# The out-projection in halves of sixteen bits, and the cuts of weights and rows shared out anew among three engines

## The reference

```python
x = x + attention(layernorm(x), ctx, ctx, Wq, Wk, Wv, Wfc, bfc)   # 32 heads of 16, 8 groups of keys; "@ Wfc.T + bfc" is the out-projection
x = x + ffn(layernorm(x), gate_weight, gate_w, up_w, down_w, sh_gate_w, sh_up_w, sh_down_w)

def ffn(h):                                   # h: 2048 rows of 512
    scores = softmax(h @ gate_weight.T)       # 8 experts in 4 groups, the best 2 groups, in them the best 2 experts
    wmat = weights of the two chosen experts, 0 for the others
    routed = sum over e of wmat[:, e] * ((silu(h @ gate_w[e].T) * (h @ up_w[e].T)) @ down_w[e].T)      # width 352
    shared = (silu(h @ sh_gate_w.T) * (h @ sh_up_w.T)) @ sh_down_w.T                                    # width 704
    return routed + shared
```

## Time and profile before

| | us |
|---|---|
| device time, median of 3 runs | 774.12 (771.83 to 774.58) |
| profiled execution, its own time | 773.04 |
| span of its instructions | 771.3 |
| TensorE busy in the span | 748.0 (97%) |
| VectorE | 567.5 (74%) |
| ScalarE | 424.4 (55%) |
| GpSimd | 267.4 (35%) |

### The profile page before, as it was taken

How to read it: one execution, slowest core, us unless ns; L and a number is a source line. 1 busy time by engine, 2 the same in 40 slices (tenths; PEclk the granted TensorE clock), 3 DMA queues, 4 the chain that set the end, 5 groups by cost and what they waited for, 6 DMA issues and landing times.

```text
span 771.3 us, 15970 instructions
## 1 busy us (share of the span) xinstructions
PE 748.0 (97%) x5151; PEld 404.5 (52%) x5152; DVE 567.5 (74%) x1194; ACT 424.4 (55%) x860; POOL 267.4 (35%) x222
## 2 busy tenths in 40 slices
PE   6998999999999999999999999999999999999997
PEld 4553533444444335666655656555555555555554
DVE  5777779999999977887689886555555555446767
ACT  3666568988888875776624543343434343323231
POOL 3263007999995303657000101111111111016331
PEclk9999989999999999999999999999999999999999
DMA  9898846575655799996678556777777779549995
GB/s 331 336 406 252 252 158 202 170 208 170 181 178 158 248 356 331 367 381 224 192 203 243 138 134 160 178 180 177 180 177 177 180 180 216 128 110 280 306 259 164
DMA packets 161336, 171.04 MB, mean 222 GB/s; under 512 B 103616, under 2 KB 117440, under 8 KB 160768
## 3 DMA queue, kind: packets, MB, share of 16 engines
q1 hardware_dynamic: 149724, 128.36, 57.0%
q0 software_dynamic: 10960, 40.90, 17.1%
...
## 4 chain that ended last, share of the span: by engine, by line
PE 77%; DVE 13%; DMA 5%; issue 2%; ACT 2%; SPq 1%; ACTq 0%; DVEq 0%
PE psum L1500 31%; PE psum L1512 17%; DVE sb_rows L1732 6%; PE psum L1430 5%; PE psum L1349 5%; PE psum L1239 4%; PE psum L1335 4%; PE psum L1263 3%; DMA sb_weights<-in_wdn 2%; PE psum L1215 2%; DMA sb_weights<-in_x 1%; PE psum L1366 1%; PE psum L1448 1%; PE psum L1220 1%; DMA x_dram<-sb_rows 1%
## 5 line engine op out<-in xcount | busy, mean ns | idle before, releaser
L1500 PE MATMUL psum<-sb_weights,sb_rows 128*128 (+1 forms) x1608 | 250.8, 313 | 0.0
L1500 PEld LDWEIGHTS psum<-sb_weights,sb_rows 128*128 128x128 f16 x1608 | 157.3, 98 | 91.1 <-DMA sb_rows<-xnT_dram 0.3
L1732 DVE TENSOR_REDUCE sb_rows<-psum 128x4 f32<-128x1024 f32 x128 | 149.9, 1215 | 5.4 <-PE psum L1263 5.4
L1054 ACT ACTIVATE sb_weights<-psum 128x512 f32<-128x512 f32 x256 | 139.2, 595 | 23.5 <-PE psum L1335 20.5
L1512 PE MATMUL psum<-sb_weights,sb_hT 128*128 (+1 forms) x630 | 147.2, 379 | 0.0
...
L1512 PEld LDWEIGHTS psum<-sb_weights,sb_hT 128*128 128x128 f16 x630 | 61.6, 98 | 64.8
L1128 ACT ACTIVATE psum<-psum 128x352 f32<-128x352 f32 x71 | 31.8, 448 | 114.4 <-DVE psum L1986 104.0
L1335 PE MATMUL psum<-sb_weights 50*128 50x512 f16 x256 | 87.0, 390 | 2.3 <-ACT sb_weights L1054 1.4
L1349 PE MATMUL psum<-sb_weights 128*32 128x256 f32 x1024 | 83.1, 397 | 0.3
L1263 PE MATMUL psum<-sb_weights 48*128 48x256 f16 x512 | 71.8, 275 | 0.7 <-DVE sb_rows L1732 0.7
L1986 DVE SCALAR_TENSOR_TENSOR psum<-psum,sb_inv_now,sb_h 128x352 f32<-128x352 f32 x39 | 23.1, 593 | 49.0 <-issue 40.1
...
...
## 6 DMA issues: line engine op xcount, KB each, us to landing
...
slot_y<-sb_rows SPq DMA_DIRECT2D x39, 256.0 KB, 2.3
...
x_dram<-sb_rows SPq DMA_DIRECT2D x24, 256.0 KB, 4.2
q_parts<-sb_weights SPq DMA_DIRECT2D x16, 256.0 KB, 4.0
sb_rows<-in_x POOLq DMA_DIRECT2D x16, 256.0 KB, 5.4
```

The source lines that it names most:

```text
L1054: nc.scalar.activation(probs[G % 2][:, kt, pair * 512:(pair + 1) * 512], bank[4 + f % 2], ACT.Exp, scale=exp_by[n]).then_inc(exp_done, 1)
L1500: mm = nc.tensor.matmul(bank[GU_BANKS[par][which]][:, 0:F], x_T[:, xp * D + k * P:xp * D + (k + 1) * P], gu(wp, k, which), start=(k == 0 a ...
L1732: nc.vector.tensor_reduce(to[:, :, j // UB, :, j % UB, qt], psum[:, banks[qt] * 512:(banks[qt] + 2) * 512] .rearrange("p (a h k) -> p a h ...
```

## The change

1. **The out-projection in float16.** Wfc (4 tiles of 128x512) is loaded early; its scale comes from a sum of squares that GpSimd makes in the projections' time (8 products and sums of 128x512 and smaller), ScalarE squares the values (`v_square`) for a scale of attention's rows; `cut_fc` (GpSimd, attention) cuts Wfc in 4 x 3 instructions. `ot_evac` writes the high part with the scale, VectorE makes the low part (`out_low`, one instruction of 128x512 for a tile), and TensorE does 12 float16 products for a tile: eight with the high part, then, behind a wait for `out_low`, four with the low part. The residual sum becomes one instruction with a factor.
2. **Held experts.** Four instead of five: GpSimd cuts 12 halves in attention instead of 10. The remaining eight halves all go to VectorE (`second_part` in the tiles 2, 4, 5, 7, 8, 10, 11 and 13). SyncE loads them.
3. **Normed rows.** `cut_rows` goes from VectorE to GpSimd, which also issues the store of the rows; the shared down matrices are cut by GpSimd around the tiles 12 and 14.
4. **Shared down scales by squares.** The last two `dn_abs_max` go; GpSimd sums the squares of the two matrices instead (`shared_sum`, 10 instructions each) between its bias sums, and VectorE takes the result in `shared_tops`.
5. **The seam.** The first two `ot_transpose` are issued two steps earlier, the last `normalise` stands inside the first `residual_norm`, bias sums go in pairs of tiles, the ring has one turn of five buffers and three more, and the register loads come before attention.

The diff, cut to what matters (places in SBUF, the ring's order, the squares of Wfc and `load_scales` are left out):

```diff
-HELD = 5
+HELD = 4
 CUTS_P2 = CUTS - 2 * HELD
+HELD_TILES = (2, 4, 5, 7, 8, 10, 11, 13)
+SHARED_TILES = (12, 14)
...
+                    if (n, l) == (2, 0):
+                        sp.dma_start(wfc_words, wfcT.rearrange("p k n -> p (k n)")).then_inc(fc_ld, 16)
...
+                if u == 12:
+                    sp.wait_ge(fc_cut, CUT_SEEN + FC_STEPS * KD)
+                    for c in range(SH):
+                        load_shared_down(c)
+                for i in {12: (0, 1), 13: (2, 3, 4)}.get(u, ()):
...
+            bias_order = list(range(1, TILES // 2)) + [0]
+            squares, SUM_STEPS, SUMS_SEEN = units[:, 0:DN_W], 10, SQUARE_SEEN + 2 * KD + 7
+            def shared_sum(c):
+                raw, done = dn_raw((NE + c) % 3), SUMS_SEEN + SUM_STEPS * c
+                nc.gpsimd.tensor_tensor(squares, raw, raw, ALU.mult).then_inc(fc_square, 1)
+                n, done = DN_W // 2, done + 1
+                pool.wait_ge(fc_square, done)
+                while n > NF:
+                    nc.gpsimd.tensor_tensor(squares[:, 0:n], squares[:, 0:n], squares[:, n:2 * n], ALU.add).then_inc(fc_square, 1)
+                    n, done = n // 2, done + 1
+                    pool.wait_ge(fc_square, done)
+                nc.gpsimd.tensor_tensor(dn_sums[:, c, :], squares[:, 0:NF], squares[:, NF:2 * NF],
+                                        ALU.add).then_inc(fc_square, 1)
+                pool.wait_ge(fc_square, done + 1)
...
-                if i >= 2:
-                    pool.wait_ge(xb_st[i % 2], i // 2 * 16)
-                nc.gpsimd.dma_start(xb_sb[i % 2], x_tiles[bias_order[i]]).then_inc(xb_ld[i % 2], 16)
+                if i > 0:
+                    pool.wait_ge(xb_st, i * 16)
...
+            def cut_fc(k):
+                scale = w_scale[:, FC_COL:FC_COL + 1].broadcast_to([P, D])
+                nc.gpsimd.tensor_tensor(wfc16[:, k, 0, :], wfc_raw[k], scale, ALU.mult).then_inc(fc_cut, 1)
+                pool.wait_ge(fc_cut, CUT_SEEN + FC_STEPS * k + 1)
+                nc.gpsimd.tensor_tensor(wfc_raw[k], wfc_raw[k], scale, ALU.mult).then_inc(fc_cut, 1)
+                pool.wait_ge(fc_cut, CUT_SEEN + FC_STEPS * k + 2)
+                nc.gpsimd.tensor_tensor(wfc16[:, k, 1, :], wfc_raw[k], wfc16[:, k, 0, :], ALU.subtract).then_inc(fc_cut, 1)
+            pool.wait_ge(w_fc, 32)
             load_x(0)
             for t in range(TILES):
+                if t < KD:
+                    cut_fc(t)
                 if t < CUTS_P2:
-                    pool.wait_ge(nm_done, t + 3)
+                    pool.wait_ge(nm_done, t * 5 // 6 + 3)
                     cut_weights(t)
-                if t + 1 < TILES:
-                    load_x(t + 1)
-                add_bias(t)
-            def dn_second(e, count, pieces):
+                if t in (TILES - 3, TILES - 1):
+                    c = (t - TILES + 3) // 2
+                    pool.wait_ge(sh_ld, 16 * SH)
+                    shared_sum(c)
+                if t == TILES - 1:
+                    nc.gpsimd.memset(units[:, 0:2 * FP], 0.0).then_inc(h_zero, 1)
+                if t % 2 == 0:
+                    add_bias(t // 2)
+                elif t + 1 < TILES:
+                    load_x(t // 2 + 1)
...
-            pool.wait_ge(attn_done, UNITS * UG)
-            pool.wait_ge(dn_max_done, NE + SH)
-            for h in range(3):
-                load_held(h)
-            for c in range(CUTS_P2, CUTS):
-                h = c - CUTS_P2
-                if h % 2 == 0:
-                    scale_weights(c)
-                    second_part(c)
-                else:
-                    pool.wait_ge(gu_cut_v, h // 2 + 1)
-                if h + 3 < 2 * HELD:
-                    load_held(h + 3)
-            for c in range(SH):
-                dn_second(NE + c, c + 1, [dn_raw((NE + c) % 3)])
...
+            def cut_rows(t):
+                s = t % 2
+                pool.wait_ge(lnt_evac, t + 1)
+                nc.gpsimd.tensor_tensor(ln16[s][:, D:2 * D], lnT[s], ln16[s][:, 0:D], ALU.subtract).then_inc(ln16_done, 1)
+                pool.wait_ge(ln16_done, t + 1)
+                nc.gpsimd.dma_start(xnT_dram[t], ln16[s]).then_inc(lnt_stored[s], 16)
+            for t in range(TILES):
+                cut_rows(t)
+                if t + 2 in SHARED_TILES:
+                    c = SHARED_TILES.index(t + 2)
+                    dn_scaled_part(NE + c, c + 1, dn_raw((NE + c) % 3))
+                if t + 1 in SHARED_TILES:
+                    c = SHARED_TILES.index(t + 1)
+                    dn_low(NE + c, c + 1, dn_raw((NE + c) % 3))
...
+            def v_square(n):
+                nc.scalar.activation(bank[5], bank[5], ACT.Square,
+                                     accum_out=half_max[:, 2 * V_COLS + n:2 * V_COLS + n + 1]).then_inc(v_free, 1)
...
-                nc.scalar.copy(oT[s], bank[s][:].rearrange("p (k t) -> p k t", k=KD)).then_inc(ota_evac, 1)
+                nc.scalar.activation(oT[s][:, 0], bank[s][:].rearrange("p (k t) -> p k t", k=KD), ACT.Copy,
+                                     scale=out_scale(t)).then_inc(ota_evac, 1)
...
+            ot_evac(1, 1)
             attn_out(UNITS * UG - 1)
             nc.scalar.activation(warm, ident[:, 0:TPB], ACT.Sqrt)
+            ot_evac(2, 0)
             for t in range(2):
-                ot_evac(t + 1, (t + 1) % 2)
...
-                if t - 2 < 2 * HELD:
-                    first_part(t - 2)
-                if t == 2:
+                if t in HELD_TILES:
+                    first_part(HELD_TILES.index(t))
...
-                    mm = nc.tensor.matmul(bank[2 + s][:], oT[s][:, k, :], wfc_sb[:, k, :],
-                                          start=(k == 0), stop=(k == KD - 1))
+                    for wp in range(2):
+                        nc.tensor.matmul(bank[2 + s][:], oT[s][:, 0, k, :], wfc16[:, k, wp, :],
+                                         start=(k == 0 and wp == 0), stop=False)
+                pe.wait_ge(ot_cut, t + (LOW_SEEN + 1))
+                for k in range(KD):
+                    mm = nc.tensor.matmul(bank[2 + s][:], oT[s][:, 1, k, :], wfc16[:, k, 0, :],
+                                          start=False, stop=(k == KD - 1))
...
+            out_project(0, 0)
+            pair_transpose(LAST - 1)
+            ot_transpose(2, 2, 0)
+            out_project(1, 1)
+            pe.wait_ge(dn_max_done, NE + 1)
...
+            def out_low(t):
+                dve.wait_ge(ota_evac, t + 1)
+                nc.vector.scalar_tensor_tensor(oT[t % 2][:, 1], bank[t % 2][:].rearrange("p (k t) -> p k t", k=KD), out_scale(t),
+                                               oT[t % 2][:, 0], ALU.mult, ALU.subtract).then_inc(ot_cut, 1)
+            def shared_tops():
+                dve.wait_ge(fc_square, SQUARE_SEEN + 2 * KD + 7 + 10 * SH)
+                link(nc.vector.tensor_reduce(dn_max[:, NE:NE + SH], dn_sums, AX.X, ALU.max))
+                nc.vector.tensor_scalar(dn_max[:, NE:NE + SH].bitcast(I32), dn_max[:, NE:NE + SH].bitcast(I32), 0.5, float(127 << 22),
+                                        ALU.mult, ALU.add).then_inc(dn_max_done, 1)
+            out_low(0)
+            shared_tops()
+            out_low(1)
+            dve.wait_ge(scale_done, 1)
+            link(nc.vector.tensor_scalar(fc_inv, w_inv[:, V_COLS:V_COLS + 2], w_inv[:, FC_COL:FC_COL + 1], X_SCALE * X_SCALE,
+                                         ALU.mult, ALU.mult))
...
-            dn_abs_max(2 * UG)
-            dn_abs_max(2 * UG + 1)
-            normalise(UNITS * UG - 2)
-            def cut_rows(t, s):
-                dve.wait_ge(lnt_evac, t + 1)
-                nc.vector.scalar_tensor_tensor(ln16[s][:, D:2 * D], bank[4 + s], X_SCALE, ln16[s][:, 0:D],
-                                               ALU.mult, ALU.subtract).then_inc(ln16_done, 1)
...
-                nc.vector.tensor_tensor(x2_sb[s], bank[2 + s][:], residual, ALU.add).then_inc(x2_done, 1)
+                nc.vector.scalar_tensor_tensor(x2_sb[s], bank[2 + s][:], fc_inv[:, t // EARLY:t // EARLY + 1], residual,
+                                               ALU.mult, ALU.add).then_inc(x2_done, 1)
                 dve.wait_ge(x2_done, t + 1)
                 link(nc.vector.bn_stats(stats[:, 0, :], x2_sb[s]))
                 link(nc.vector.bn_aggr(mv[:, s, :], stats[:, 0, :]))
                 nc.vector.tensor_scalar(var_e[:, 0:1], mv[:, s, 1:2], EPS, None, ALU.add).then_inc(var_done, 1)
-                if not (isinstance(t, int) and t < 2):
-                    cut_rows(t - 2, s)
+                if t == 0:
+                    normalise(UNITS * UG - 2)
+                elif t + 1 < TILES:
+                    out_low(t + 1)
...
-                residual_norm(t, t % 2, t // 2)
-                if t % 2 == 1 and t < 2 * HELD + 2:
-                    second_part(t - 2)
-            cut_rows(TILES - 2, 0)
+                if t > 2:
+                    residual_norm(t, t % 2, t // 2)
+                if t in HELD_TILES:
```

(1 more changed line is left out.)

308 lines of the change are left out of this document (171 added, 137 removed).

## The result

The changed kernel takes 788.27 us (median of 4 runs, 786.88 to 791.05) beside 772.98 for the kernel before: ratio 1.0207, 95% interval 1.0177 to 1.0238, slower by 15 to 16 us. The forecast was 778.0 in a range of 767 to 786. The sign of the likeliest case was right, its size (5.0) a third of what came, and the time lies outside the range. The profiled execution took 787.37, its span is 785.6, 14.3 more than before.

A forecast was written before the change was run, and what follows sets the result against it. TensorE was taken to bound the token stage, VectorE close behind; +6.7 (GpSimd wait) - 4.2 (token stage) + 1.0 (tail) - 0.5 (register loads) + 2.0 (clock) = +5.0 on 773.04, so 778.0, range 767 to 786.

The forecast's parts named there:

- the likeliest case: Whole kernel: the terms' sum, +5.0 on 773.04, so 778.0, own range 774.5 to 782; chance 0.45.
- TensorE in the token stage: Out-projection: twelve float16 products take 2.59 instead of 3.44 to 3.55, a tile needs 4.3, 0.9 less.
- VectorE from the fifth tile on: Token stage: VectorE late next, 3.64 a tile plus eight held cuts of 1.59; 71.0 against 75.3, -4.2.
- Rival C: Token stage: `cut_rows` on GpSimd holds up held cuts, each staying at 2.6; 8 x 1.0, 786; chance 0.15.
- A: Seam: GpSimd not last if sums give back 2.7, pairs 3.6, landings 3.1; end 285.9, time 767; chance 0.18.
- B: Seam: both landings at 3.8, GpSimd ends at 293.6, no clock loss; 774, same; chance 0.22.
- GpSimd through attention: Attention to seam: GpSimd's new work ends at 295.3, VectorE waits, x2 of tile 0 at 296.8 instead of 290.07, +6.7.
- The last landing: GpSimd ahead of the second `shared_sum`: last load's landing uncovered, 3.1 and 0.7 for twice the size, 3.8.
- about 1.1 (six small steps): VectorE in the token stage: the scales of the down matrices, booked within the 71.0.
- The clock: Start of token stage: after TensorE's idle, half clock for some 4 us of work, +2.0 (0 to 2.5).
- The tail: Behind the last x2: gate 13 and `ln_transpose` 14 still on TensorE's list, +1.0 (0 to 2).
- Attention, "0" and "-0.5": ScalarE's squares beside projections cost 0 (up to +1); register loads moved ahead give -0.5 (0 to -1.2).

The follow-up runs named there:

- e5_rows_vector: Changed kernel with the low part of the normed rows subtracted by VectorE again for 14 of 16 tiles, GpSimd only issuing the store: 799.71 us, ratio 1.0344.
- e10_pool_held: Changed kernel with all mends and VectorE's first low parts made earlier, plus three of eight held halves cut by GpSimd: 776.17 us, ratio 1.0027.
- e3_scales_early: Changed kernel with the gathering of the down matrices' largest values one tile earlier, as in the kernel before: 782.91 us, ratio 1.0123.

## Why the prediction was wrong

- **TensorE in the token stage**, 2.59 for twelve products: right (2.60 from the first of them to the gate behind the last, at full clock).
- **VectorE from the fifth tile on**: right. From 325 to 365 VectorE is busy 92% of the time, TensorE 94%. 3.68 in a tile without a held cut (3.64), 5.17 with one, or 5.67 where `out_low` waited 0.46 for ScalarE's copy; held cut 1.68 (1.67). Rival C didn't come in the changed kernel; e5_rows_vector and e10_pool_held show that it was near: a held cut beside GpSimd's work took 4.52 and 3.85 against 1.68. The Trainium skill (SBUF — State Buffer, "Who interferes with whom") says that a VectorE instruction with two SBUF inputs contends with a GpSimd instruction that reads SBUF, over a port pair that one holds and the other waits for; the traces agree, both cuts ended 1.5 behind GpSimd's instruction.
- **Rivals A and B** fell by GpSimd's rows. Of A's three conditions one came in part: squaring ran at 1.66 ns a column (2.76 for 1536 columns), and a sum of squares took 8.4 where A had 7.9. The bias pairs ran at the forecast's 2.09 (2.35 each), and neither landing was 3.1. B's landings of 3.8 did not come either.
- **GpSimd through attention**, +6.7: the mechanism and nearly every term right; the step that failed here is the size of one term. The last landing, "uncovered too (3.1 and 0.7 for twice the size, 3.8)", measured 8.7. The 3.1 is the median of four loads, of which three were issued before the ring's first loads of 768 KB (254.33 in the kernel before); the row of 5.26 was issued beside two of them (265.80). That the ring's traffic makes the landing long is likely and not shown. With 8.7 the working gives x2(0) at 300.1 (from 296.8 + 4.9 - 1.6 for the shorter sums), measured 300.04. That the cuts ended only 0.6 from the forecast is partly luck: their chain started 1.8 sooner (117.4 in place of 119.2) and took 1.2 longer (144.0 in place of 142.8).
- **The step that failed outright**: the start of the stage. I booked the gathering of the scales as "about 1.1 (six small steps)" on VectorE and missed that the change moves it one tile back (behind the third `residual_norm`, not the second; neither the list of the change nor its diff above shows this) while TensorE's `ln_transpose` of tile 1 still waits for it. That wait is 4.1 idle us and one more fall of the clock. From the first sum to the last the stage took 76.7, with the clock in it, against a forecast of 71.0 and 2.0 for the clock; e3_scales_early gives 4.0 of these back, and 6.5 in all. No rival contained it.
- **The clock**, +2.0 (0 to 2.5): too small. With fillers in four waits 3.3 came back inside the stage (5.6 in all): two falls between 300 and 320, not one, and both lie on the path, because VectorE waits for TensorE there (2.64 and 3.88 us).
- **The tail**, +1.0: measured 2.5. The lateness itself is 1.1, from the last sum to the first product of the shared expert (3.3 in place of 2.2), as forecast; that product at half clock adds 1.7 (5.42 against 3.74), and 0.3 comes back ahead of the second. Whether the clock falls there differs between profiles of like kernels.
- **Attention, "0" and "-0.5"**: it starts 2.0 sooner, loses 1.9 to its 57th output, where the wait for small transfers lies, and 1.3 more in its last two units. The first two cancel by luck, and none of them set the time here, since the first residual sum waited for GpSimd; of the three only the early start helped it.

By the sum: +10.0 for the first residual sum against +6.7 with -0.5; +4.9 - 3.5 = +1.4 for the stage against -4.2 + 2.0 = -2.2; +2.5 and 0.4 behind it against +1.0. In all +14.3 against +5.0.
